# Two of four key tiles of a weighed product in high and low halves, with new places for the parts around them

## The chip, the cores and the metric

One core of a Trainium2 chip runs the whole program. The metric is the device time of one execution in microseconds (us), lower is better. Five engines work side by side, each through its own list of instructions in order: TensorE (PE, with its weight loads as PEld), VectorE (DVE), ScalarE (ACT), GpSimd (POOL) and SyncE (SP, which only issues DMAs). They wait for each other by semaphores.

## What is computed

Two layers over 8 sequences of 512 tokens of width 128. The first layer is a gated recurrence and a binarized feed-forward block. The second is a memory layer with 8 heads and a routed feed-forward block with 8 experts. The change touches the second layer's memory part, which in the reference is, cut down:

```
grads    = vmap(grad(chunk_loss))(mem_ws, keys, lr, values)     # 8 chunks of 64 tokens a head
momentum = assoc_scan(mom_gate, -grads)
updates  = assoc_scan(1 - decay, momentum)
w0, w1   = mem_w0 + updates[0], mem_w1 + updates[1]             # one pair of weights per chunk
x        = q @ w0
vals     = silu(x) @ w1
vals     = rmsnorm(vals) * (gamma + 1) * gate
out      = vals @ w_combine
```

A chunk's weights are sums of outer products of earlier tokens, so `q @ w0` is computed as the product with the start weights plus `(q k') * coef` applied to the tokens' gradients: a score matrix of keys against queries, weighed by a factor for each pair of chunks, and then "applied" as a product with a 128-row tile of gradients. Only queries behind the keys count, so key tile i (of 4 tiles of 128) needs 450 - 128 i query columns: 450, 322, 194 and 66.

## The kernel before

`first_layer` takes the first 127 us. `attend` then goes through 64 pairs (sequence, head) in `heads`, which calls `step(f, s, z)` on each engine: `f` is head n in its first half, `s` head n-1 in its second half, and `z` head n-2, whose result is added up. The order on each engine is the order of the code in its `step`. For 40 of the 64 steps (`s` in sequences 2 to 6) there is also one block `x` of 128 routed tokens through an expert. These are block steps; the other 24 are plain steps.

On TensorE a step is, in order: the projections U, EB and QA; the second scores of s; (block) a transpose of the block's rows; the product of s with `w1` into EB; `xs` with `w1` into VB and `apply(VB, err_t, ...)`, four products; (block) the first expert products; four transposes of `err`; the error product (`err_2` with `w4t`, into U); the first scores of f, with four transposes of `du` among them; the projection into XB and `apply(XB, du_t, ...)`; (block) the second expert products; `vals` with `w_out`; and the sums of squares.

A float32 matrix product is done in one of two ways here. A plain float32 `matmul` shows as two records in the trace. A `product` takes both operands as two parts of type float32r, high (a rounded copy) and low (the rest), and does high x high, low x high and high x low, one record each. Both `apply` calls are of the first kind: `p_sb` is the weighed score matrix that `weigh` on VectorE writes from PSUM (four operations of 512, 384, 128 and 256 columns, tile order 0, 1, 3, 2; `SC_BANKS` = 3 increments of `v_p1` or `v_p0`), and `err_t` and `du_t` are the transposed gradients that ScalarE copies out of PSUM.

The names around it: VectorE computes `q_sb` (L1109, L1111), `err_low` (L1115), `du` (L1118), the two `weigh` calls, and at the step's end the work that comes in some steps only: `coefs` (after heads 1 and 6 to 11), `blocks` (after 3), `places` (after 4), `last_sum` and `add_rows` (in the last sequence). The next step begins on VectorE with `ms` (L1074). GpSimd waits for that `ms` with `rs`, then computes `rg`, then `s_low` and `qa_low` (L1207), and later the two parts of the sum of squares, `sq_rest` (L1232) and `sq_low` (L1236). TensorE's product of s with `w1` waits for `s_low`, its error product for `err_low`.

Of the kernel before, what the change touches and what calls it, by code (L numbers as in the profile page):

```python
# [8 lines left out]
I32 = mybir.dt.int32  # L9
# [6 lines left out]
P = 128  # L16
# [11 lines left out]
E = 8  # L28
# [601 lines left out]
def attend(nc, m, a, out):  # L630

    with ExitStack() as ctx:
# [11 lines left out]
        err_t = sb("err_t", [P, T, D])  # L644
        du = sb("du", [P, S])
        du_t = sb("du_t", [P, T, D])
        p_sb = sb("p_sb", [P, P_COLS])
# [3 lines left out]
        sq_rest = sb("sq_rest", [P, QW])  # L651
# [6 lines left out]
        token_q = sb("token_q", [P, 3, NT])  # L658
# [4 lines left out]
        def carve(ap, at):  # L663
# [35 lines left out]
        a_sh, a_qh, a_eh, a_xh, a_hi, a_mid = (sem(f"a_{k}") for k in ("sh", "qh", "eh", "xh", "hi", "mid"))  # L699
        v_q, v_g, v_du, v_p0, v_p1, v_ms, v_acc, v_y, v_xl, v_el = (  # L700
            sem(f"v_{k}") for k in ("q", "g", "du", "p0", "p1", "ms", "acc", "yb", "xl", "el"))
        g_rs, g_rg, g_sl, g_ql, g_rest, g_lo = (sem(f"g_{k}") for k in ("rs", "rg", "sl", "ql", "rest", "lo"))
# [40 lines left out]
        with nc.Block() as block_:  # L743

            @block_.tensor
            def _(pe):
# [21 lines left out]
                def apply(out, rows, made, n):  # L768
                    for i in SC_ORDER:
                        if i != 3:  # L770
                            pe.wait_ge(made, SC_BANKS * n + {0: 1, 1: 2, 2: 3}[i])
                        last = pe.matmul(out[:, P * i:QW], rows[:, i, :], p_sb[:, P_COL[i]:P_COL[i] + QW - P * i],  # L772
                                         start=False, stop=True, skip_group_check=True)
                    return last

                def routing(s):
# [8 lines left out]
                    if c == 5:  # L785
                        pe.wait_ge(v_alpha, 1)
                        rows = FREE[:, 0:3 * NT].rearrange("p (a n) -> p a n", a=3)
                        pe.matmul(rows, m.ahead, m.per_token[:], start=True, stop=False)
                        pe.matmul(rows[:, :, 0:NT - 1], m.behind, m.per_token[:, :, 1:], start=False, stop=True).then_inc(p_shift, 1)

                def step(f, s, z):
# [27 lines left out]
                    if s is not None:  # L819
                        pe.wait_ge(v_acc, k)  # L820
                        pe.wait_ge(a_et, k + 1)
                        product(VB[:, 0:QW], [w[:] for w in w1], [part[:] for part in xs_2])
                        apply(VB, err_t, v_p1, k).then_inc(p_v, 1)
                    if x is not None:
# [4 lines left out]
                        last.then_inc(p_h, 1)  # L829
                    if f is not None:  # L830
# [4 lines left out]
                        last.then_inc(p_et, 1)  # L835
                        pe.wait_ge(v_el, n + 1)
# [14 lines left out]
                        pe.wait_ge(a_et, n + 1)  # L851
                        project(XB, m.w_x, f, SHIFT)
                        pe.wait_ge(a_dt, n + 1)
                        apply(XB, du_t, v_p0, n).then_inc(p_x, 1)
# [6 lines left out]
                    if s is not None:  # L861
                        pe.wait_ge(a_v, k + 1)
                        for t, r in enumerate(Q_ROWS):
                            pe.matmul(VB[0:r, t * P:t * P + P], vals[:, t * P:t * P + r], m.w_out[:, s[1], :], start=True, stop=True)  # L864
                        pe.wait_ge(g_lo, k + 1)
# [12 lines left out]
            def _(act):  # L878
                def gate_rows(c):
                    act.wait_ge(v_f, c + 1)  # L880
                    for t in range(T):
# [4 lines left out]
                def scale_rows(c):  # L886

                    act.wait_ge(v_top, 1)
                    for t in range(c * T, c * T + T):
# [3 lines left out]
                def spread(b):  # L893

                    for g in range(2):
                        nc.scalar.copy(gates_x[b % 2][g], gates[:, g, b * H:b * H + H, :].unsqueeze(2).broadcast_to([P, H, T, NC])).then_inc(a_gates, 1)

                def step(f, s, z):
# [7 lines left out]
                    if f is not None:  # L906
# [5 lines left out]
                        act.wait_ge(v_g, n)  # L912
                        nc.scalar.activation(th[:], U[:], ACT.Tanh, scale=0.5).then_inc(a_th, 1)
# [7 lines left out]
                        nc.scalar.copy(qa_2[0][:], qa[:]).then_inc(a_qh, 1)  # L921
                        act.wait_ge(p_e, n + 1)
                        act.wait_ge(p_d, n)
                        nc.scalar.copy(err[:], EB[:]).then_inc(a_err, 1)  # L924
                        act.wait_ge(a_err, n + 1)
                        nc.scalar.copy(err_2[0][:], err[:]).then_inc(a_eh, 1)
                    if s is not None:
                        act.wait_ge(p_v, k + 1)
# [481 lines left out]
```

## Time and profile before

| what | us |
|---|---|
| runs | 1109.14, 1114.12, 1114.44 (median 1114.12) |
| the profiled execution: time | 1113.32 |
| its span (first to last instruction) | 1110.8 |
| TensorE busy | 1071.7 (96%) |
| VectorE busy | 686.0 (62%) |
| ScalarE busy | 678.7 (61%) |
| GpSimd busy | 562.4 (51%) |
| one block step | 15.72 |
| one plain step | 13.73 |

The execution's time is 2.5 us above the span. Matmul records overlap in the trace: each lasts some 0.16 us longer than the distance to the next one, so costs on TensorE are read from the distance of starts, not from durations. A step's length is the distance of two starts of the first projection (`w_u_high`).

### The profile page before, as it was taken

The page shows a single profiled execution, that of the slowest core. Times are in us where ns is not written, and L with a number is a line of the kernel's source. Part 1 is how long each engine was busy: PE and PEld are TensorE (multiplying, and loading weights), DVE is VectorE, ACT ScalarE, POOL GpSimd, SP SyncE. Part 2 cuts the span into 40 slices and gives each one's busy share as a digit, 9 for nine tenths or more (in the row PEclk, how much of TensorE's full clock was granted, in tenths as well). Part 3 has the DMA queues.
Part 4 walks back from the last instruction along what each step waited for, and adds up shares of the span by engine and source line. Part 5 has one row for each costly group of instructions (what it writes and reads, how often), then busy time and mean ns, then how long its engine had stood idle before and what let it go on. Part 6 is the DMA issues. An engine that isn't in the chain of part 4 may idle for free. (4 is left out here: it accounts for less than half of the span.)

```text
span 1110.8 us, 19052 instructions
## 1 busy us (share of the span) xinstructions
PE 1071.7 (96%) x6613; PEld 900.1 (81%) x6613; DVE 686.0 (62%) x1752; ACT 678.7 (61%) x1356; POOL 562.4 (51%) x574
## 2 busy tenths in 40 slices
PE   6899799999999999999999999999999999999994
PEld 4666588888888888888888888888888888888883
DVE  5887566767766555565556555565556555657774
ACT  5776466677655656565556555665566565656663
POOL 6885244478874444344434444444434443444553
PEclk9999699999999999999999999999999999999997
DMA  7210300000030000000000000000000000012221
GB/s 205 79 46 29 105 1 1 1 15 30 21 97 12 19 10 9 8 21 10 9 8 11 20 11 8 9 20 11 8 8 11 20 8 6 6 42 61 69 70 42
DMA packets 42129, 32.66 MB, mean 29 GB/s; under 512 B 4042, under 2 KB 36652, under 8 KB 41900
## 3 DMA queue, kind: packets, MB, share of 16 engines
q1 hardware_dynamic: 38484, 25.93, 8.0%
q0 software_dynamic: 2304, 4.74, 1.3%
q8 instruction: 54, 0.88, 0.3%
q10 hardware_dynamic: 1248, 0.79, 0.2%
q14 instruction: 39, 0.32, 0.1%
HBM read 18.30 MB, written 13.41 MB: 29 GB/s over the span
## 5 line engine op out<-in xcount | busy, mean ns | idle before, releaser
L1040 DVE TENSOR_TENSOR p_sb<-bank,coef 128x512 f32<-128x512 f32 (+3 forms) x512 | 218.8, 483 | 3.1 <-PE bank L749 2.6
L1232 POOL TENSOR_TENSOR sq_rest<-sq,sq_high 128x450 f32<-128x450 f32 x64 | 67.2, 1050 | 245.1 <-ACT sq_high L934 245.1
L772 PE MATMUL bank<-p_sb,err_t 128*128 128x450 f32 (+3 forms) x512 | 132.9, 402 | 0.2 <-DVE p_sb L1040 0.2
L772 PE MATMUL bank<-p_sb,du_t 128*128 128x450 f32 (+3 forms) x512 | 128.8, 394 | 0.0
L772 PEld LDWEIGHTS bank<-p_sb,err_t 128*128 128x128 f32 x512 | 83.7, 190 | 45.5 <-DVE p_sb L1040 25.2
L1236 POOL TENSOR_TENSOR sq_low<-sq_rest,sq_mid 128x450 bf16<-128x450 f32 x64 | 67.6, 1056 | 96.5 <-ACT sq_mid L948 96.2
L772 PEld LDWEIGHTS bank<-p_sb,du_t 128*128 128x128 f32 x512 | 82.1, 190 | 41.4 <-issue 23.9
L1093 DVE SCALAR_TENSOR_TENSOR acc<-bank,rg,acc 128x128 f32<-128x128 f32 x224 | 62.9, 343 | 68.2 <-POOL rg L1220 68.2
L1118 DVE SCALAR_TENSOR_TENSOR du<-q_sb,bank 128x512 f32<-128x512 f32 x64 | 44.0, 688 | 87.7 <-PE bank L749 87.7
L1216 POOL TENSOR_TENSOR rs<-ms,neg_half 128x4 f32<-128x4 f32 x64 | 80.6, 1259 | 28.6 <-DVE ms L1075 27.3
L1207 POOL TENSOR_TENSOR s_low<-s_sb,s_high 128x512 fp32r<-128x512 f32 x64 | 82.7, 1293 | 20.2 <-ACT s_high L911 20.1
L909 ACT ACTIVATE s_sb<-bank 128x512 f32<-128x512 f32 x64 | 38.3, 598 | 88.4 <-PE bank L749 88.3
L903 ACT ACTIVATE xs<-bank 128x450 f32<-128x450 f32 x64 | 35.0, 547 | 89.0 <-PE bank L772 89.0
L930 ACT COPY vals<-bank 128x450 f32<-128x450 f32 x64 | 34.3, 536 | 89.3 <-PE bank L772 89.3
L1126 DVE TENSOR_TENSOR xl_all<-bank,xl_all 128x128 f32<-128x128 f32 x40 | 11.7, 293 | 117.2 <-PE bank L858 117.2
L1246 POOL DMA_INDIRECT ffn_rows<-xl_all,ids x40 | 41.5, 1039 | 83.9 <-DVE xl_all L1126 83.9
L1207 POOL TENSOR_TENSOR qa_low<-qa,qa_high 128x450 fp32r<-128x450 f32 x64 | 74.5, 1165 | 12.3 <-ACT qa_high L921 12.0
L924 ACT COPY err<-bank 128x512 f32<-128x512 f32 x64 | 37.6, 587 | 62.6 <-PE bank L749 62.6
L864 PE MATMUL bank<-w_out,vals 128*128 128x128 f32 (+1 forms) x512 | 67.4, 274 | 0.6 <-ACT vals L930 0.6
L864 PEld LDWEIGHTS bank<-w_out,vals 128*128 128x128 f32 (+1 forms) x512 | 60.0, 179 | 0.9 <-ACT vals L930 0.9
L945 ACT COPY du_t<-bank 128x512 f32<-128x512 f32 x64 | 37.6, 587 | 36.2 <-PE bank L848 36.2
L764 PE MATMUL bank<-qa,yb 128*128 128x66 f32 (+1 forms) x256 | 52.9, 288 | 0.0
(297 smaller groups left out, 3103.1 us busy)
## 6 DMA issues: line engine op xcount, KB each, us to landing
sorted_rows<-coef SPq DMA_DIRECT2D x5, 516.0 KB, 5.0
rows<-sorted_rows SPq DMA_DIRECT2D x40, 64.5 KB, 1.8
x<-in_L_attn_inputs SPq DMA_DIRECT2D x8, 256.0 KB, 5.5
x_rows<-x SPq DMA_DIRECT2D x8, 256.0 KB, 2.3
ew<-in_L_ffn_w SPq DMA_DIRECT2D x8, 256.0 KB, 3.9
attn_out<-acc SPq DMA_DIRECT2D x7, 256.0 KB, 2.1
ew<-attn_out SPq DMA_DIRECT2D x7, 256.0 KB
ew<-ffn_rows SPq DMA_DIRECT2D x8, 192.0 KB
```

What stands on the lines that cost most here:

```text
L764: last = pe.matmul(out, left[:, (i - 2) * P:(i - 1) * P], right[:, P * i:], start=True, stop=True)
L772: last = pe.matmul(out[:, P * i:QW], rows[:, i, :], p_sb[:, P_COL[i]:P_COL[i] + QW - P * i], start=False, stop=True, skip_group_check=True)
L864: pe.matmul(VB[0:r, t * P:t * P + P], vals[:, t * P:t * P + r], m.w_out[:, s[1], :], start=True, stop=True)
L909: nc.scalar.activation(s_sb[h % 2][:], U[:], ACT.Silu).then_inc(a_s, 1)
L1040: last = nc.vector.tensor_tensor(dst, src, w, ALU.mult)
L1093: last = nc.vector.scalar_tensor_tensor(sums, o, g, sums, ALU.mult, ALU.add)
L1118: nc.vector.scalar_tensor_tensor(du[:], q_sb[:], 0.5, U[:], ALU.mult, ALU.mult).then_inc(v_du, 1)
L1207: nc.gpsimd.tensor_tensor(parts[1][:], whole[:], parts[0][:], ALU.subtract).then_inc(done, 1)
L1216: nc.gpsimd.tensor_tensor(rs[:], ms[:], m.neg_half[:, 0:T], ALU.pow).then_inc(g_rs, 1)
L1232: nc.gpsimd.tensor_tensor(sq_rest[:], sq[:], sq_3[0][:], ALU.subtract).then_inc(g_rest, 1)
L1236: nc.gpsimd.tensor_tensor(sq_3[2][:], sq_rest[:], sq_3[1][:], ALU.subtract).then_inc(g_lo, 1)
L1246: nc.gpsimd.indirect_dma_start(m.ffn_rows, bass.IndirectOffsetOnAxis(ids[r][:, 0:1], axis=0), y[r], None).then_inc(s_y[r], 16)
```

## The change

- `apply` is gone. `apply_plain` does key tiles 3 and 2 as before (full float32). `apply_halves` does tiles 0 and 1 in halves: for each, high p with high and low rows, then low p with high rows.
- New operations per head and side (there are two sides, err with `v_p1` and du with `v_p0`): ScalarE makes the high parts of `p_sb` (450 and 322 columns, `p_high_of`). The low parts come from GpSimd on the err side (semaphore `g_l1`) and from VectorE on the du side (`p_low_of`, `v_l0`). `err_t` and `du_t` are split: tiles 2 and 3 stay float32, tiles 0 and 1 become pairs `errt2` and `dut2`. For `errt2` ScalarE first copies PSUM into `th`, and at the end of its step makes the high part; VectorE makes the low part (`v_etl`).
- On TensorE the transposes of `err` stand between the narrow and the halved tiles on the err side, and the output rows (`vals` with `w_out`) on the du side. The block's first expert products stand ahead of `apply_plain`.
- `du` is now `err`'s buffer, `sq_rest` is `sq`, `token_q` and `per_token` lie in `amd`. ScalarE's row work (`gate_rows`, `scale_rows`) is cut in two pieces, and the first two scatters of GpSimd come after the new low parts. `ids` moves towards the end of VectorE's step.

The diff, cut to its core:

```diff
+                def apply_plain(out, rows, made, n):
+
+                    pe.wait_ge(made, SC_BANKS * n + 3)
+                    for i in (3, 2):
+                        pe.matmul(out[:, P * i:QW], rows[:, i - 2, :], p_sb[:, P_COL[i]:P_COL[i] + QW - P * i],
+                                  start=False, stop=True, skip_group_check=True)
+
+                def apply_halves(out, halves, n, high, low, lows):
+
+                    for i in (0, 1):
+                        cols = QW - P * i
+                        p_high, p_low = (part[:, QW * i:QW * i + cols] for part in p_2)
+                        pe.wait_ge(high, 2 * n + i + 1)
+                        if lows == 3:
+                            pe.wait_ge(low, 3 * n + 1)
+                        for rows in halves:
+                            pe.matmul(out[:, P * i:QW], rows[:, i, :], p_high, start=False, stop=True, skip_group_check=True)
+                        pe.wait_ge(low, lows * n + lows - 1 + i)
+                        last = pe.matmul(out[:, P * i:QW], halves[0][:, i, :], p_low, start=False, stop=True, skip_group_check=True)
                     return last
...
+                def p_high_of(made, n, i, done):
+
+                    cols = QW - P * i
+                    act.wait_ge(made, SC_BANKS * n + i + 1)
+                    nc.scalar.copy(p_2[0][:, QW * i:QW * i + cols], p_sb[:, P_COL[i]:P_COL[i] + cols]).then_inc(done, 1)
...
                         nc.scalar.copy(qa_2[0][:], qa[:]).then_inc(a_qh, 1)
+                    if s is not None:
+                        p_high_of(v_p1, k, 0, a_p1)
+                    if f is not None:
                         act.wait_ge(p_e, n + 1)
                         act.wait_ge(p_d, n)
                         nc.scalar.copy(err[:], EB[:]).then_inc(a_err, 1)
+                    if s is not None:
+                        p_high_of(v_p1, k, 1, a_p1)
...
                         weigh(f, p_s0, v_p0, n, s)
+                        dve.wait_ge(a_dt, n + 1)
+                        nc.vector.tensor_tensor(du_t2[1][:].rearrange("p t d -> p (t d)"), EB[:, 0:2 * D],
+                                                du_t2[0][:].rearrange("p t d -> p (t d)"), ALU.subtract).then_inc(v_l0, 1)
+                        p_low_of(a_p0, n, 0, v_l0)
+                        p_low_of(a_p0, n, 1, v_l0)
+                        dve.wait_ge(a_et, 2 * n + 2)
+                        flat = [part[:].rearrange("p t d -> p (t d)") for part in err_t2]
+                        nc.vector.tensor_tensor(flat[1], th[:, 0:2 * D], flat[0], ALU.subtract).then_inc(v_etl, 1)
...
+                        for i in (0, 1):
+                            cols = QW - P * i
+                            high, low = (part[:, QW * i:QW * i + cols] for part in p_2)
+                            pool.wait_ge(a_p1, 2 * k + i + 1)
+                            nc.gpsimd.tensor_tensor(low, p_sb[:, P_COL[i]:P_COL[i] + cols], high, ALU.subtract).then_inc(g_l1, 1)
```

TensorE in a block step, from the product of `xs` with `w1` (`xs_high` against `w1n_high`) to the error product (`err_high` against `w4t_high`). Before:

```order
L749 MATMUL bank<-xs_high,w1n_low 128x450
L772 MATMUL bank<-p_sb,err_t 128x450 [waits v_p1]
L772 MATMUL bank<-p_sb,err_t 128x322 [waits v_p1]
L772 MATMUL bank<-p_sb,err_t 128x66
L772 MATMUL bank<-p_sb,err_t 128x194 [waits v_p1]
L828 MATMUL bank<-xl_all 128x128 [waits a_qa,v_xf]
L828 MATMUL bank<-xl_all 128x128 x3
L834 MATMUL bank<-ident,err 128x128 [waits a_xs,a_err]
L834 MATMUL bank<-ident,err 128x128 x3
L749 MATMUL bank<-err_high,w4t_high 128x512 [waits v_q,v_el]
```

The same stretch now:

```order
L749 MATMUL bank<-xs_high,w1n_low 128x450
L839 MATMUL bank<-xl_all 128x128 [waits a_qa,v_xf]
L839 MATMUL bank<-xl_all 128x128 x3
L772 MATMUL bank<-p_sb,err_t 128x66 [waits v_p1]
L772 MATMUL bank<-p_sb,err_t 128x194
L847 MATMUL bank<-ident,err 128x128 [waits a_xs,a_err]
L847 MATMUL bank<-ident,err 128x128 x3
L784 MATMUL bank<-p_high,errt_high 128x450 [waits a_p1,v_etl]
L784 MATMUL bank<-p_high,errt_low 128x450
L786 MATMUL bank<-p_low,errt_high 128x450 [waits g_l1]
L784 MATMUL bank<-p_high,errt_high 128x322 [waits a_p1]
L784 MATMUL bank<-p_high,errt_low 128x322
```

The halved tiles stand right ahead of the error product, and the expert products that stood behind the applies stand ahead of them.

GpSimd in the same step, where `s_low` and `qa_low` are what TensorE needs early and `ffn_rows` is the block's result. Before:

```order
L1216 TENSOR_TENSOR rs<-ms,neg_half 128x4 [waits v_ms]
L1220 TENSOR_TENSOR rg<-rs,lr_gate 128x4 [waits v_acc,g_rs]
L1207 TENSOR_TENSOR s_low<-s_sb,s_high 128x512 [waits a_sh]
L1207 TENSOR_TENSOR qa_low<-qa,qa_high 128x450 [waits a_qh]
L1232 TENSOR_TENSOR sq_rest<-sq,sq_high 128x450 [waits p_o,a_hi]
L1236 TENSOR_TENSOR sq_low<-sq_rest,sq_mid 128x450 [waits g_rest,a_mid]
```

Now:

```order
L1279 TENSOR_TENSOR rs<-ms,neg_half 128x4 [waits v_ms]
L1283 TENSOR_TENSOR rg<-rs,lr_gate 128x4 [waits v_acc,g_rs]
L1270 TENSOR_TENSOR s_low<-s_sb,s_high 128x512 [waits a_sh]
L1270 TENSOR_TENSOR qa_low<-qa,qa_high 128x450 [waits a_qh]
L1295 TENSOR_TENSOR p_low<-p_sb,p_high 128x450 [waits a_p1]
L1295 TENSOR_TENSOR p_low<-p_sb,p_high 128x322 [waits a_p1]
L1301 TENSOR_TENSOR sq<-sq,sq_high 128x450 [waits p_o,a_hi]
L1305 TENSOR_TENSOR sq_low<-sq,sq_mid 128x450 [waits g_rest,a_mid]
```

Two operations have come in between `qa_low` and the squares.

VectorE at the end of the same step and the start of the next, from the last weighed tile to `ms`. Before:

```order
L1040 TENSOR_TENSOR p_sb<-bank,coef 128x256 [waits p_s0]
L1126 TENSOR_TENSOR xl_all<-bank,xl_all 128x128 [waits p_yy]
L1067 TENSOR_LOAD blk_e
L1067 ISA x2
L1069 ISA [waits v_yx]
L1069 COPY xl_all<-ew 128x646
L1074 TENSOR_SCALAR ms<-bank 128x3 [waits g_rs,p_o]
```

Now:

```order
L1087 TENSOR_TENSOR p_sb<-bank,coef 128x256 [waits p_s0]
L1176 TENSOR_TENSOR dut_low<-bank,dut_high 128x256 [waits a_dt]
L1097 TENSOR_TENSOR p_low<-p_sb,p_high 128x450 [waits a_p0]
L1097 TENSOR_TENSOR p_low<-p_sb,p_high 128x322 [waits a_p0]
L1182 TENSOR_TENSOR errt_low<-thu,errt_high 128x256 [waits a_et]
L1187 COPY ids<-rows 128x1 [waits s_y0,s_rows0]
L1189 TENSOR_TENSOR xl_all<-bank,xl_all 128x128 [waits p_yy]
L1122 TENSOR_LOAD blk_e
```

Four operations stand between `weigh` and the step's end. In a plain step the blocks' rows are absent, and `coefs` or one of the others follows the fourth.

## Rows read from the trace of the kernel before

**Rows 1.** The page: busy time by engine, and TensorE's granted clock in 40 slices.

```profile
PE 1071.7 (96%) x6613; PEld 900.1 (81%) x6613; DVE 686.0 (62%) x1752; ACT 678.7 (61%) x1356; POOL 562.4 (51%) x574
...
PEclk9999699999999999999999999999999999999997
```

**Rows 2.** Windows: stretch, length, busy time (x instructions) of the engines, PEclk, DMA.

```profile
503.80:519.52 15.72, 15.72 (x107) 13.55 (x105) 8.93 (x24) 9.30 (x19) 6.98 (x8) 1.00 0.03 9
266.25:279.98 13.73, 13.73 (x91) 11.67 (x88) 10.19 (x21) 8.87 (x18) 11.39 (x12) 1.00 0.06 20
```

**Rows 3.** Timeline of PE in one block step: start us, us, engine, line, operation.

```profile
503.80 0.48 PE L749 MATMUL bank<-y_high,w_u_high 128*128 128x512 f32 x1
...
508.33 0.36 PE L749 MATMUL bank<-xs_high,w1n_high 128*128 128x450 f32 x1
508.53 0.37 PE L749 MATMUL bank<-xs_low,w1n_high 128*128 128x450 f32 x1
...
508.97 2.12 PE L772 MATMUL bank<-p_sb,err_t 128*128 128x450 f32 x8
...
512.17 0.48 PE L749 MATMUL bank<-err_high,w4t_high 128*128 128x512 f32 x1
...
513.57 0.31 PE L749 MATMUL bank<-qa_high,y_high 128*128 128x322 f32 x1
513.71 0.31 PE L749 MATMUL bank<-qa_low,y_high 128*128 128x322 f32 x1
...
515.57 2.01 PE L772 MATMUL bank<-p_sb,du_t 128*128 128x450 f32 x8
```

**Rows 4.** The same timeline, cut behind the fourth record of the du apply.

```profile
515.57 1.46 PE L772 MATMUL bank<-p_sb,du_t 128*128 128x450 f32 x4
```

**Rows 5.** Timeline of DVE in the same block step.

```profile
508.23 1.68 DVE L1040 TENSOR_TENSOR p_sb<-bank,coef 128x512 f32<-128x512 f32 x4
509.82 0.68 DVE L1109 SCALAR_TENSOR_TENSOR q_sb<-bank,s_sb 128x512 f32<-128x512 f32 x1
510.54 0.69 DVE L1111 SCALAR_TENSOR_TENSOR q_sb<-thu,q_sb 128x512 f32<-128x512 f32 x1
511.15 0.68 DVE L1115 TENSOR_TENSOR err_low<-err,err_high 128x512 fp32r<-128x512 f32 x1
```

**Rows 6.** Timelines of POOL and ACT in the same block step.

```profile
506.11 1.29 POOL L1207 TENSOR_TENSOR s_low<-s_sb,s_high 128x512 fp32r<-128x512 f32 x1 [0.19 <-ACT s_high L911]
507.64 1.15 POOL L1207 TENSOR_TENSOR qa_low<-qa,qa_high 128x450 fp32r<-128x450 f32 x1 [0.23 <-ACT qa_high L921]
...
506.99 0.57 ACT L921 CAST qa_high<-qa 128x450 fp32r<-128x450 f32 x1
```

**Rows 7.** Timelines of POOL and DVE in a plain step, where the two overlap.

```profile
229.70 1.15 POOL L1207 TENSOR_TENSOR qa_low<-qa,qa_high 128x450 fp32r<-128x450 f32 x1
...
229.41 0.68 DVE L1109 SCALAR_TENSOR_TENSOR q_sb<-bank,s_sb 128x512 f32<-128x512 f32 x1
230.12 1.29 DVE L1111 SCALAR_TENSOR_TENSOR q_sb<-thu,q_sb 128x512 f32<-128x512 f32 x1
```

**Rows 8.** Timelines at the step's end with `places`: DVE, then POOL, then PE.

```profile
206.34 0.16 DVE L1015 TENSOR_TENSOR ew<-ew 128x8 f32<-128x8 f32 x1
...
210.95 0.15 DVE L1074 TENSOR_SCALAR ms<-bank 128x3 f32<-128x3 f32 x1
...
212.80 1.27 POOL L1207 TENSOR_TENSOR s_low<-s_sb,s_high 128x512 fp32r<-128x512 f32 x1
...
209.48 0.47 PE L749 MATMUL bank<-y_high,w_u_high 128*128 128x512 f32 x1
...
214.12 0.50 PE L749 MATMUL bank<-s_high,w1n_high 128*128 128x512 f32 x1 [0.39 <-POOL s_low L1207]
```

**Rows 9.** Timelines of DVE with `coefs`, `blocks` and `last_sum`.

```profile
263.11 0.68 DVE L985 TENSOR_TENSOR_SCAN ew<-ew 128x256 f32<-128x256 f32 x1
263.83 1.48 DVE L987 TENSOR_TENSOR_SCAN coef<-ew 128x256 f32<-128x256 f32 x1
...
192.62 0.68 DVE L1003 TENSOR_TENSOR_SCAN ew<-restart,ew 128x256 f32<-128x256 f32 x1
...
196.08 0.16 DVE L1074 TENSOR_SCALAR ms<-bank 128x3 f32<-128x3 f32 x1
...
1058.13 1.92 DVE L1157 SCALAR_TENSOR_TENSOR ew<-ew,token_q 128x128 f32<-128x128 f32 x4
```

More of the change, by code:

```diff
@@ L643, in attend @@
         err, err_2 = sb("err", [P, S]), pair("err2", [P, S])
[L644 to L647, printed above, removed]
+        err_t, err_t2 = sb("err_t", [P, 2, D]), pair("errt2", [P, 2, D])
+        du = err
+        du_t, du_t2 = sb("du_t", [P, 2, D]), pair("dut2", [P, 2, D])
+        p_sb, p_2 = sb("p_sb", [P, P_COLS]), pair("p2", [P, 2 * QW - P])
         xs, xs_2 = sb("xs", [P, QW]), pair("xs2", [P, QW])
@@ L787, in routing @@
                         rows = FREE[:, 0:3 * NT].rearrange("p (a n) -> p a n", a=3)
-                        pe.matmul(rows, m.ahead, m.per_token[:], start=True, stop=False)
+                        pe.matmul(rows, m.ahead, m.per_token, start=True, stop=False)
                         pe.matmul(rows[:, :, 0:NT - 1], m.behind, m.per_token[:, :, 1:], start=False, stop=True).then_inc(p_shift, 1)
@@ L884, in gate_rows, with scale_rows @@
                     last.then_inc(a_g, 1)
-                def scale_rows(c):
+                def scale_rows(c, tiles):
                     act.wait_ge(v_top, 1)
-                    for t in range(c * T, c * T + T):
+                    for t in (c * T + t for t in tiles):
                         last = nc.scalar.mul(m.xl_all[:, t, 0:D], m.xl_all[:, t, 0:D], m.rr[:, 2, t:t + 1])
@@ L896, in spread, with rows_of @@
                         nc.scalar.copy(gates_x[b % 2][g], gates[:, g, b * H:b * H + H, :].unsqueeze(2).broadcast_to([P, H, T, NC])).then_inc(a_gates, 1)
+                def rows_of(s, tiles):
+                    k, c = n_of(s), last_head(s)
+                    if c is not None and c > 0:
+                        gate_rows(c - 1, tiles)
+                    if 1 <= k <= B:
+                        scale_rows(k - 1, tiles)
                 def step(f, s, z):
@@ L924, in step @@
                         nc.scalar.copy(err[:], EB[:]).then_inc(a_err, 1)
+                    if s is not None:
+                        p_high_of(v_p1, k, 1, a_p1)
+                    if f is not None:
                         act.wait_ge(a_err, n + 1)
                         nc.scalar.copy(err_2[0][:], err[:]).then_inc(a_eh, 1)
+                    if x is not None:
+                        act.wait_ge(p_h, x + 1)
+                        for k4 in range(FB):
+                            last = nc.scalar.activation(hid[:, k4, :], QA[:, k4 * P:k4 * P + P], ACT.Relu, bias=w1s[:, PAR + 2 + k4:PAR + 3 + k4])
+                        last.then_inc(a_h, 1)
                     if s is not None:
+                        rows_of(s, (0, 1))
                         act.wait_ge(p_v, k + 1)
@@ L1042, in weigh, with p_low_of @@
                             last.then_inc(done, 1)
+                def p_low_of(made, n, i, done):
+                    cols = QW - P * i
+                    p = p_sb[:, P_COL[i]:P_COL[i] + cols]
+                    dve.wait_ge(made, 2 * n + i + 1)
+                    high, low = (part[:, QW * i:QW * i + cols] for part in p_2)
+                    nc.vector.tensor_tensor(low, p, high, ALU.subtract).then_inc(done, 1)
                 def plain_keys(b):
@@ L1167, in finish_batch @@
                     q = (B - 1) % 2
[L1168 removed]
+                    dve.wait_ge(a_g, 2 * B)
                     dve.wait_ge(v_acc, B * H)
```

89 lines of the change are left out of this document (46 added, 43 removed).

## The prediction, made before the changed kernel had run

> **What bounds the kernel now.** I read the page first. TensorE is busy for 96% of the span at the full clock, the other engines for 51 to 62% [rows 1]. The windows say the same of one step: in a block step TensorE is busy for all of 15.72 us, in a plain one for all of 13.73, and PEclk is 1.00 in both [rows 2]. So a microsecond taken off TensorE counts, as long as nobody else comes late. The slack of the others has to be read from their order, not from their busy share. One wait is visible on TensorE: the err apply is 2.12 long where the same eight records on the du side are 2.01 [rows 3], so some 0.13 in each block step goes into waiting for the first weighed tile (0.03 in a plain one).
>
> I take times in a block step from its first projection, at 503.80 [rows 3].
>
> **TensorE's own work.** Tiles 0 and 1 of one apply are four records: 1.46 less the tail of 0.16 (a 450-column record lasts 0.37 where the next begins 0.20 later [rows 3, 4]) is 1.30 us. A float32r product of 450 columns takes 0.20 to 0.205 and one of 322 takes 0.15 [rows 3], three of each are 1.065. That saves 0.23 per apply, 0.46 per step, **29.4 us over 64 steps**. Tiles 2 and 3 stay as they are, and no product is added elsewhere. The weight loads go from two to three per tile, and each lies beside a product of at least 0.15.
>
> **Small waits.** On the err side `apply_plain` now wants all four weighed tiles. They end at 509.91, which is 6.11 [rows 5]; TensorE, which now does the block's 0.89 us first, comes at 6.03, so 0.13 remains. On the du side the last weighed tile needs scores that end only 0.6 us earlier, so some 0.05 is new. Plain steps get 0.05 there and some 0.14 at the halved du tiles. Against before that is +0.05 per block step and +0.16 per plain step: **+5.8 us**.
>
> **The low parts on GpSimd.** This is the term that I expect to decide. In a block step the first weighed tile is done at 5.11, ScalarE's high part takes the 0.57 of `qa_high` [rows 6] and is there at 5.73, and GpSimd's low part at 1.15 for 450 columns runs from 5.77 to 6.92 [rows 6]. The second, 322 columns, is 1.15 less 128 x 0.0022 (the slope between 1.29 for 512 and 1.15 for 450 [rows 6]), 0.88. VectorE at that time does the second `q_sb` (from 6.74) and `err_low` (from 7.35) [rows 5]. Both read two tensors from SBUF, and so does GpSimd. What happens then is in the trace: `q_sb` takes 0.69 alone [rows 5], but 1.29 when it starts at 230.12 while GpSimd's `qa_low` runs from 229.70 to 230.85 [rows 7]. It ends 0.56 after GpSimd's end, that is it did its work only once GpSimd let go, 0.13 before its end. The first `q_sb`, which reads PSUM, took its usual 0.68 beside it [rows 7]. There are eight such steps.
>
> So the four operations go one after the other: GpSimd 450 until 6.92; `q_sb` until 7.48; GpSimd 322 (held back until 0.13 before that) until 8.25; `err_low`, which asks last, until 8.80. If GpSimd's second came ahead of `q_sb`, the sum and the end would be nearly the same (8.9). TensorE would be at its error product at 8.22 (8.45 before, less 0.23) and gets `err_low` at 8.87: a wait of 0.65 in each of 40 block steps, **+26 us**. The low part itself, at 8.30, lies within that. In a plain step the products come 0.89 earlier and GpSimd follows `qa_low` at once: low part until 6.1, `q_sb` until 6.65, low part until 7.4, `err_low` until 7.97, TensorE would be there at 7.13 and waits 0.91: 24 x 0.91, **+21.8 us**. Bounds: nothing, if the operations overlap freely (`err_low` is then ready at 8.03, as before), and 0.8 per block step and 1.1 per plain step if the order is the worst. I take the worked values, since the eight rows show the same engines, the same operations and the same sizes.
>
> The Trainium skill says the same kind of thing more strictly: SBUF — State Buffer, section "Who interferes with whom", holds that a VectorE instruction with two SBUF inputs and a GpSimd instruction that reads SBUF exclude each other for the whole instruction. By that the 0.13 of overlap at each of three handovers is lost too, and the sum would be some 25 us higher; the row shows the 0.13, and I go by the row.
>
> **The end of VectorE's step.** New there are four operations after `weigh`: 256 columns, 450, 322 and 256, about 0.42 + 0.62 + 0.54 + 0.49. They wait for ScalarE's high parts, which stand behind `sq_mid`, and the 450 one meets GpSimd's `sq_low` as above. Laid out, a plain step's last one ends 0.15 us before the step does; before, `weigh` ended about 3 us before. In block steps there are 1.1 us more (the second expert products and the rest), so nothing is late there. In plain steps whatever follows is pushed into the next step: `coefs` 2.15 (7 steps), `blocks` 3.46 (1), `places` 4.6 (1) [rows 8, 9], `last_sum` 1.92 (7), with `add_rows` and its wait 2.5 (6 of those 7). Behind them stand `ms`, then GpSimd's `rs`, `rg` and `s_low`, for which TensorE waits. The trace has one such case: with `places` `ms` came 1.47 after the step's first projection, `s_low` ended at 214.07, and TensorE lost 0.98 by then [rows 8]. So the loss is `ms`'s delay less 0.5, and it spares 0.2 of the wait at `err_low`. With the delay equal to the work less 0.15: coefs 1.3 x 7 = 9.0, blocks 2.6, places 3.75 - 0.98 = 2.8, last_sum alone 1.0, with add_rows 1.6 - 0.29 = 1.3 x 6 = 7.8. Together **+23 us** (15 to 32; none, if VectorE's end came over 2.5 us sooner than I lay it out).
>
> **Ends.** In the first step `choose` is pushed back by 2, in the last the halves come one after another, +1: **+3 us**.
>
> **The sum.** 1113.3 - 29.4 + 5.8 + 26 + 21.8 + 23.2 + 3 = 1163.7 for the profiled execution's time (its span is 2.5 less). The median is 0.8 above that execution, so I say 1164. Its own range is 1140 to 1182.
>
> **Rivals.** (1) TensorE stays the bound everywhere: the four operations overlap, and the end of VectorE's step is absorbed. For it speaks that every engine has several us of idle time in a step [rows 2]; against it the 1.29 of rows 7. It gives 1113.3 - 29.4 + 5.8 = 1090 (1084 if the small waits go as well). (2) No exclusion at `err_low`, but the end of the step works as laid out, without the meeting with `sq_low`: 1113.3 - 29.4 + 5.8 + 22 + 3 = 1115, no change. It turns slower than before where the pushed work exceeds 20 us. (3) Exclusion as forecast, but the pushed work finds room: 1113.3 + 24.2 + 3 = 1140. That holds if `sq_mid` and ScalarE's high parts come 1 us sooner. (4) The halved tiles don't run as one-record products at 0.205. The saving is then gone and everything else stands: over 1190. The existing products are of just this form, so this is unlikely.
>
> **How the numbers follow.** Forecast 0.50, rival 3 (still slower) 0.16, rival 2 0.14, rival 1 0.16, rival 4 and worse 0.04. Rival 2 lies half within 0.5% and half to its sides (0.5% is about what a measurement of this kernel can tell from no change): same 0.09, faster 0.18, slower 0.73. The range of 8 in 10 leaves out rival 1 and the worst: 1106 to 1184.
>
> **What would show it.** Right: the second `q_sb` or `err_low` with means well over 0.69 and 0.68, idle time of TensorE ahead of `w4t_high` released by `err_low` (0.65 per block step, 0.9 per plain one), block steps of 15.9 to 16.0 and plain ones of 14.3, and steps of over 15.5 after heads 6 to 11 and 57 to 62 with TensorE waiting for `s_low`. Wrong: block steps of 15.3 with `err_low` at 0.68 (rivals 1 and 2), no idle time ahead of `s_low`'s product (rivals 1 and 3). TensorE's busy share should fall to some 90% if I am right and stay near 96% in rival 1. The forecast rests on one pair of waits; if GpSimd's low parts start 1 us sooner than I lay out, they are over before the second `q_sb`, and a block step is 0.4 shorter than before instead of 0.24 longer.

## The result

The changed kernel takes 1172.61 us (median of four runs, 1170.56 to 1172.97) against 1112.53 for the kernel before on the same chip: ratio 1.054, 95% interval 1.0508 to 1.0572. It is slower by 5.4%. The forecast was 1164, range 1106 to 1184. The profiled execution took 1172.53 us, 59.2 more than that of before (1113.32); its span is 1170.8.

### The profile after

The page's busy times and TensorE's granted clock of the changed kernel, against [rows 1]:

```profile
PE 1099.9 (94%) x6869; PEld 936.0 (80%) x6869; DVE 874.2 (75%) x2008; ACT 807.0 (69%) x1804; POOL 709.1 (61%) x702
...
PEclk9999799999999999999999999999999999999996
```

The clock is as before. TensorE has less work to do and yet more busy time, because a matmul record is drawn out to its modelled end and covers short waits. Steps tell more. The windows of a block step, a plain step, and a plain step behind `coefs` (stretch, length, busy time of PE, PEld, DVE, ACT, POOL, PEclk), against [rows 2]:

```profile
603.06:619.13 16.07, 15.94 (x111) 14.13 (x109) 11.80 (x27) 11.24 (x27) 9.37 (x10) 1.00 0.03 10
...
365.03:379.44 14.41, 14.09 (x94) 12.07 (x92) 11.66 (x24) 10.27 (x23) 8.06 (x8) 1.00 0.09 25
...
285.52:301.97 16.45, 14.85 (x94) 11.91 (x92) 13.50 (x26) 11.01 (x25) 13.57 (x14) 1.00 0.05 16
```

Block steps went from 15.72 to 16.07, plain ones from 13.73 to 14.41, the ones behind `coefs` from 13.73 to 16.45. The starts of the 64 first projections put the loss, 54.4 us from the first of them to the last, at 14.0 in the 40 block steps and 40.3 in the 23 other intervals; of these, 7.7 lie in four steps of the last sequence, which went from 14.07 to 16.0.

What TensorE's weight loads waited for over the whole run (us in total, times, longest):

```profile
PEld bank L749 <- DVE err_low L1166: 23.9, 63, 1.4
PEld bank L772 <- ACT du_t L989: 23.1, 64, 0.8
...
PEld bank L749 <- DVE ms L1130: 16.1, 12, 2.5
PEld bank L772 <- DVE p_sb L1087: 10.6, 52, 0.7
PEld bank L749 <- POOL s_low L1270: 9.5, 13, 1.0
PEld bank L786 <- DVE p_low L1097: 8.7, 22, 0.9
```

The wait for `err_low` was forecast, and the one for `s_low` behind a late `ms`. That TensorE would wait for `ms` itself, 16.1 us in 12 places, and for `du_t` was not. The groups of the two VectorE instructions that the forecast named, with GpSimd's low parts (busy us, mean ns):

```profile
L1295 POOL TENSOR_TENSOR p_low<-p_sb,p_high 128x450 fp32r<-128x450 f32 (+1 forms) x128 | 147.0, 1170 | 37.5 <-ACT p_high L903 36.1
...
L1166 DVE TENSOR_TENSOR err_low<-err,err_high 128x512 fp32r<-128x512 f32 x64 | 78.5, 1226 | 0.3 <-ACT err_high L967 0.3
...
L1162 DVE SCALAR_TENSOR_TENSOR q_sb<-thu,q_sb 128x512 f32<-128x512 f32 x64 | 53.0, 828 | 2.2
```

In a block step before, `err_low` took 0.68 and `q_sb` 0.69 [rows 5]. The timelines of the block step at 603.06, GpSimd first, then VectorE, the weight loads and TensorE (start us, us):

```profile
608.81 2.31 POOL L1295 TENSOR_TENSOR p_low<-p_sb,p_high 128x450 fp32r<-128x450 f32 x2 [0.77 <-ACT p_high L903]
...
609.76 0.75 DVE L1162 SCALAR_TENSOR_TENSOR q_sb<-thu,q_sb 128x512 f32<-128x512 f32 x1
610.43 1.24 DVE L1166 TENSOR_TENSOR err_low<-err,err_high 128x512 fp32r<-128x512 f32 x1
...
611.72 0.19 PEld L749 LDWEIGHTS bank<-err_high,w4t_high 128*128 128x128 f32 x1 [0.36 <-DVE err_low L1166]
...
611.18 0.41 PE L786 MATMUL bank<-p_low,errt_high 128*128 128x322 f32 x1
611.72 0.51 PE L749 MATMUL bank<-err_high,w4t_high 128*128 128x512 f32 x1
612.07 0.39 PE L749 MATMUL bank<-err_low,w4t_high 128*128 128x512 f32 x1
```

GpSimd's two low parts end at 611.12. `err_low` started at 610.43 and ends at 611.67, 0.55 behind them, where alone it takes 0.68. It did its work only when GpSimd was through, but for the last 0.13, as the `q_sb` of [rows 7]. TensorE had its last halved record at 611.18, could have gone on 0.15 later, and got `err_low` at 611.72.

### The profile page after: what moved, and what is told of

Read it like the earlier page. It is cut to its first block and busy times, and to the rows that moved or that the text cites. A ratio compares the mean times of both kernels' runs of the same rounds, so it can differ in the third digit from the quotient of the medians.

```text
span 1170.8 us, 20652 instructions
## 1 busy us (share of the span) xinstructions
PE 1099.9 (94%) x6869; PEld 936.0 (80%) x6869; DVE 874.2 (75%) x2008; ACT 807.0 (69%) x1804; POOL 709.1 (61%) x702
## 5 line engine op out<-in xcount | busy, mean ns | idle before, releaser
L903 ACT CAST p_high<-p_sb 128x450 fp32r<-128x450 f32 (+1 forms) x256 | 125.9, 519 | 79.9 <-DVE p_sb L1087 79.8
L1295 POOL TENSOR_TENSOR p_low<-p_sb,p_high 128x450 fp32r<-128x450 f32 (+1 forms) x128 | 147.0, 1170 | 37.5 <-ACT p_high L903 36.1
L1301 POOL TENSOR_TENSOR sq<-sq,sq_high 128x450 f32<-128x450 f32 x64 | 67.0, 1046 | 132.6 <-ACT sq_high L981 132.5
L1097 DVE TENSOR_TENSOR p_low<-p_sb,p_high 128x450 fp32r<-128x450 f32 (+1 forms) x128 | 101.5, 831 | 31.5 <-ACT p_high L903 31.3
L1305 POOL TENSOR_TENSOR sq_low<-sq,sq_mid 128x450 bf16<-128x450 f32 x64 | 66.9, 1046 | 62.6 <-ACT sq_mid L992 62.4
L1169 DVE SCALAR_TENSOR_TENSOR err<-q_sb,bank 128x512 f32<-128x512 f32 x64 | 44.0, 688 | 72.6 <-PE bank L749 72.6
L1166 DVE TENSOR_TENSOR err_low<-err,err_high 128x512 fp32r<-128x512 f32 x64 | 78.5, 1226 | 0.3 <-ACT err_high L967 0.3
L1162 DVE SCALAR_TENSOR_TENSOR q_sb<-thu,q_sb 128x512 f32<-128x512 f32 x64 | 53.0, 828 | 2.2
L772 PE MATMUL bank<-p_sb,err_t 128*128 128x66 f32 (+1 forms) x256 | 51.9, 326 | 0.1
L772 PEld LDWEIGHTS bank<-p_sb,du_t 128*128 128x128 f32 x256 | 33.4, 190 | 23.1 <-ACT du_t L989 23.1
```

What stands on the lines that cost most here:

```text
L772: pe.matmul(out[:, P * i:QW], rows[:, i - 2, :], p_sb[:, P_COL[i]:P_COL[i] + QW - P * i], start=False, stop=True, skip_group_check=True)
L903: nc.scalar.copy(p_2[0][:, QW * i:QW * i + cols], p_sb[:, P_COL[i]:P_COL[i] + cols]).then_inc(done, 1)
L1097: nc.vector.tensor_tensor(low, p, high, ALU.subtract).then_inc(done, 1)
L1166: nc.vector.tensor_tensor(err_2[1][:], err[:], err_2[0][:], ALU.subtract).then_inc(v_el, 1)
L1295: nc.gpsimd.tensor_tensor(low, p_sb[:, P_COL[i]:P_COL[i] + cols], high, ALU.subtract).then_inc(g_l1, 1)
L1301: nc.gpsimd.tensor_tensor(sq[:], sq[:], sq_3[0][:], ALU.subtract).then_inc(g_rest, 1)
```

## The experiments

All ratios are against runs of the kernel before on the same chip. "The changed kernel" is 1172.6 us. An "interval" is the distance of two starts of the first projection.

### 1. Is the wait GpSimd's doing? `err_low` from PSUM

```diff
-  nc.vector.tensor_tensor(err_2[1][:], err[:], err_2[0][:], ALU.subtract).then_inc(v_el, 1)
+  nc.vector.tensor_tensor(err_2[1][:], EB[:], err_2[0][:], ALU.subtract).then_inc(v_el, 1)
```

`EB` is the PSUM bank that `err` was copied from, so the values are the same, and the instruction has one SBUF input in place of two. First in the changed kernel, then in the kernel before.

> The changed kernel with one operand moved: err_low is computed as EB (still in PSUM) minus err_high, not err (in SBUF) minus err_high. Same values, same place, same size; it only no longer reads two tensors from SBUF. Theory (VectorE and GpSimd exclude each other when both read two SBUF tensors): err_low back from 1.24 to 0.68 us, ready about 0.55 us sooner; TensorE is then held by GpSimd's low part of tile 1 itself, so a block step falls from 16.09 to about 15.7 and a plain one from 14.4 to about 14.0. 40 x 0.4 + 24 x 0.4 = 26 us less, 1146 us, between 1138 and 1152. Rival (err_low is late because ScalarE's high parts push err_high back, or because weigh is late): nothing changes, 1172.

> The kernel before with the same one operand moved. There GpSimd is idle during err_low, so the theory expects no change: within 2 us of the kernel before, err_low at 0.68 us. A rival that reading PSUM is faster in itself would show a gain here too.

Measured: 1147.31 us, ratio 1.0302 (1.0274 to 1.0329), and 1113.61, ratio 0.9998 (0.9979 to 1.0017). The group of `err_low` in the first:

```profile
L1166 DVE TENSOR_TENSOR err_low<-bank,err_high 128x512 fp32r<-128x512 f32 x64 | 43.3, 677 | 0.0
```

One operand was changed; GpSimd's low parts ran in the same place as before (1147 and 1198 ns on average, 1146 and 1193 in the changed kernel) and VectorE's instruction went from 1226 to 677 ns beside them. In the kernel before it takes 0.683 from either source, so reading PSUM is not faster in itself. So the wait comes from two SBUF inputs meeting GpSimd, and neither from ScalarE's high parts nor from the order. It is worth 25.3 us in the changed kernel and nothing in the kernel before. Block steps fell to 15.67, plain ones to 14.0.

The timeline of TensorE in a block step of the first shows what it waits for now, and what a wait costs beside its length:

```profile
585.39 0.31 PE L784 MATMUL bank<-p_high,errt_low 128*128 128x322 f32 x1
585.54 0.41 PE L786 MATMUL bank<-p_low,errt_high 128*128 128x322 f32 x1
585.79 0.39 PE L749 MATMUL bank<-err_high,w4t_high 128*128 128x512 f32 x1
586.03 0.39 PE L749 MATMUL bank<-err_low,w4t_high 128*128 128x512 f32 x1
```

The last halved record takes 0.25 instead of 0.15, because its weight load had to wait for GpSimd's second low part and starts only as the record does, at 585.54. (In plain steps the record also starts 0.35 late.) That lay hidden in the wait for `err_low`. And the error product's first record takes 0.24 here, 0.35 where TensorE stood before it (611.72 to 612.07 above): after that wait the first record costs some 0.1 more.

I put this down to the weight load. Here it starts 0.15 ahead of its record (585.64 against 585.79), so it runs beside the record before; after the wait both start at 611.72. The kernel before shows that no wait is needed for it. There the same product stands behind four short transposes, its load starts only 0.03 ahead of the record of 512.17 [rows 3], and the record takes 0.31 with TensorE never idle:

```profile
512.14 0.19 PEld L749 LDWEIGHTS bank<-err_high,w4t_high 128*128 128x128 f32 x1
...
512.48 0.40 PE L749 MATMUL bank<-err_low,w4t_high 128*128 128x512 f32 x1
```

In the changed kernel the first halved record stands behind these transposes and takes 0.29 (610.19 to 610.48) instead of 0.205, so that cost has moved, and the 0.35 at the error product comes on top. The three pairs fit; no run changes the lead of a load by itself.

### 2. One side at a time

The err side alone: `du_t` whole again, and the old `apply` for it. The du side alone: the same for `err_t`, with no low parts on GpSimd.

```diff
-                        apply_plain(XB, du_t, v_p0, n)
+                        apply(XB, du_t, v_p0, n).then_inc(p_x, 1)
...
-                        apply_halves(XB, du_t2, n, a_p0, v_l0, 3).then_inc(p_x, 1)
```

> Only the err side (VB) is in halves; the du side is one full float32 apply at its old place, without its four VectorE operations and ScalarE copies. Theory: TensorE saves 0.23 per step, the wait at err_low stays (0.65 per block step, 0.9 per plain one), the end of VectorE's step is short again, so the steps after heads 6 to 11 and 57 to 62 lose their extra wait for s_low. 40 x 0.4 + 24 x 0.7 + 2 = 35 above before: 1148 us, block steps 16.1, plain steps 14.4, all plain steps alike within 0.4. Rival (the loss is the du side's VectorE work alone): 1105 to 1113.

> Only the du side (XB) is in halves, low parts on VectorE; the err side is one full float32 apply at its old place, without GpSimd's low parts. Theory: no wait at err_low; block steps 15.72 - 0.23 + 0.05 = 15.55, plain ones 13.7, but the pushed end of VectorE's step stays, with steps over 15 after heads 6 to 11 and 57 to 62: 1113 - 8 + 24 + 3 = 1132 us. Rival (only the exclusion costs anything, VectorE's end of the step finds room): 1113 - 15 = 1098 to 1105.

Measured: err side 1149.62 us, ratio 1.032 (1.0291 to 1.0349), with block steps of 16.07 as in the changed kernel and plain ones of 14.35. The time was as expected, but the plain steps are not alike within 0.4: 15.0 to 15.2 behind heads 7 to 10, 15.0 in the last sequence, 16.0 behind head 6 and 17.1 with `places`. I put that down to `errt_low`, the one of VectorE's four new operations that this kernel keeps. Du side 1146.11, ratio 1.0279 (1.0242 to 1.0315), 14 above what was expected, all of it in the block steps (15.97). Both sides lose by themselves. The miss on the du side has a row of its own, here the weight loads in a block step of that kernel, with ScalarE behind:

```profile
581.40 0.19 PEld L749 LDWEIGHTS bank<-y_high,w_x_high 128*128 128x128 f32 x1 [0.51 <-ACT err_t L984]
...
578.08 1.14 ACT L971 ACTIVATE xl_all<-bank,xl_all 128x128 f32<-128x128 f32 x4 [2.25 <-PE bank L849]
579.10 0.56 ACT L977 COPY vals<-bank 128x450 f32<-128x450 f32 x1
...
580.77 0.58 ACT L984 COPY err_t<-bank 128x512 f32<-128x512 f32 x1
```

ScalarE waits 2.25 for the block's first expert products (L849), to do their ReLUs, and `vals`, the squares and `err_t` queue behind them. The changed kernel can afford that order, because its TensorE does these products ahead of the err apply; my kernel had put the products back and left ScalarE's order. Two further runs follow this up.

### 3. Both leads followed up, and the wait called `du_t`

The err side alone with `err_low` from PSUM; the du side alone with the ReLUs behind the `err_t` copy as before; and the changed kernel with `err_low` from PSUM and the plain du tiles moved:

```diff
-                        pe.wait_ge(a_dt, n + 1)
-                        apply_plain(XB, du_t, v_p0, n)
...
                     if f is not None:
+                        pe.wait_ge(a_dt, n + 1)
+                        apply_plain(XB, du_t, v_p0, n)
                         apply_halves(XB, du_t2, n, a_p0, v_l0, 3).then_inc(p_x, 1)
```

> The err side alone in halves, and err_low reads the error in PSUM. In the err side alone (1149.6 us) TensorE waits 0.41 for err_low in a block step, as in the changed kernel. If that wait is the exclusion between GpSimd's low parts and a VectorE instruction with two SBUF inputs, and nothing else comes late in its place: err_low back at 0.68, block steps 15.66 instead of 16.07, plain steps 13.95 instead of 14.35, the steps after heads 6 to 11 down by about as much, and 1149.6 - 0.40 x 64 = 1124 us. If the du side were needed for the wait, 1149. The err side in halves would still be slower than the kernel before (1113): it keeps the late low part of tile 1 and its errt_low behind the weighing.

> The du side alone came to 1146.1, 14 above its expectation, all of it in the block steps (15.97 instead of 15.55). Its trace shows TensorE at the XB projection 0.51 late for ScalarE's err_t copy: ScalarE does the block's ReLUs ahead of vals there, as in the changed kernel, while TensorE still does the block's first products behind the err apply, as before. Here only that is undone: the ReLUs go behind the err_t copy again. If the miss came from this mixture, block steps are 15.55 to 15.6 and the time 1146.1 - 0.4 x 40 = 1130 us. If it came from the du side's own work (two copies on ScalarE, low parts on VectorE), it stays at 1146. What is left above 1113 - 0.2 x 64 = 1100 in the first case is the end of VectorE's step, pushed into the next one after heads 6 to 11, places and last_sum.

> Changed kernel with err_low from PSUM (1147.3), and TensorE does the plain du tiles 2 and 3 right ahead of the halved ones, behind the second expert products and the output rows. In 1147.3 TensorE waits at those plain tiles for the last weighed tile of the du side: 0.16 more between the projection's last product and the first plain record than its 0.20, in each step. If that is all that the wait costs, it goes, since the tiles are weighed 2 us earlier than they are then wanted: block steps 15.51 instead of 15.67, plain 13.85 instead of 14.0, 1147.3 - 0.16 x 64 = 1137 us. If TensorE then only waits as much longer for p_low of the du side, which is what ends last in plain steps, block steps gain and plain ones don't: 1141.

Measured: 1127.21 us, ratio 1.0117 (1.01 to 1.0133), block steps 15.67, plain 13.95, as expected step by step and 3 above in all. The GpSimd effect doesn't need the du side.

The second came to 1136.31, ratio 1.0193 (1.0176 to 1.021). The mixture explains 10 of the 14; `err_t` is ready in time and the XB projection no longer waits. But block steps are 15.72 and not 15.55 to 15.6, the same length as before, although an apply is shorter. Its weight loads say where that went:

```profile
578.99 0.52 PEld L780 LDWEIGHTS bank<-p_sb,du_t 128*128 128x128 f32 x4 [0.34 <-ACT du_t L988]
```

This is the wait that stands with 23.1 us in the list of the changed kernel. The profile names `du_t`, since one weight load has two conditions, the copy and the last weighed tile. In the changed kernel's block step the copy (ScalarE) ends at 615.06, the weighing (VectorE) at 615.17, and the load starts at 615.28:

```profile
613.42 1.75 DVE L1087 TENSOR_TENSOR p_sb<-bank,coef 128x512 f32<-128x512 f32 x4
...
614.68 0.38 ACT L989 COPY du_t<-bank 128x256 f32<-128x256 f32 x1
...
615.28 0.52 PEld L772 LDWEIGHTS bank<-p_sb,du_t 128*128 128x128 f32 x4 [0.34 <-ACT du_t L989]
...
614.96 0.37 PE L749 MATMUL bank<-y_high,w_x_low 128*128 128x450 f32 x1
615.32 0.79 PE L772 MATMUL bank<-p_sb,du_t 128*128 128x66 f32 x4
```

From the projection's last product to the first plain record it is 0.36, where the product takes 0.20: a wait of 0.16. I read it as the last weighed tile, since the copy was there 0.22 ahead and the tile 0.11; no run tells the two apart. The third kernel takes it away, whichever it is: 1138.82 us, ratio 1.0213 (1.0193 to 1.0234), 8.5 below the kernel without the move. Block steps are 15.45, 0.22 shorter, the wait and the 0.07 that the first records after it cost. The narrow tiles' own records, x4, went from 0.79 above to 0.72:

```profile
587.55 0.72 PE L772 MATMUL bank<-p_sb,du_t 128*128 128x66 f32 x4
```

Plain steps stay at 14.0: there the same time is spent at the halved tiles, where the wait for `p_low` on VectorE goes from 9.9 to 15.9 us in all. Of the two outcomes written down, the time (1137 and 1141) lies between them, the steps say the second.

### 4. Without the step's end: halves in block steps alone

What is lost outside the block steps is put down, so far by argument only, to VectorE's new work at the step's end. The last pair tests that. It puts the du side in halves in the 40 block steps alone, everything else as before, and beside it in every step. Both have the plain du tiles moved and the ReLUs as before, and the old err side.

```diff
-                    if f is not None:
+                    if f is not None and x is not None:
                         pe.wait_ge(a_dt, n + 1)
                         apply_plain(XB, du_t, v_p0, n)
                         apply_halves(XB, du_t2, d_at(n), a_p0, v_l0, 3).then_inc(p_x, 1)
```

(`x is not None` marks a block step; the same condition stands at ScalarE's high parts and VectorE's low parts.)

> Halves on the du side alone and in the 40 block steps alone, with the plain du tiles right ahead of the halved ones and the ReLUs behind the err_t copy; the err side and the 24 plain steps are the kernel before's. Where the du side was in halves in every step (1136.3), the block steps were as long as before (15.72), with 0.16 of waiting for the last weighed tile ahead of the plain tiles, and the loss of 23 us lay in the other steps: 15.1 after heads 6 to 11 and in the last sequence against 13.7 and 14.1, 17.9 against 15.2 with places. If that loss is VectorE's low parts pushing coefs, places and last_sum into the next step, it is gone here: plain steps 13.73, after heads 6 to 11 13.73, last sequence 14.07. The block steps should be 15.72 - 0.16 to 15.72 - 0.22, so 1113.4 - 40 x 0.19 = 1106 us, ratio 0.993. If the halves lose their 0.2 to another wait, 1113.

> The same with the du side in halves in every step. Block steps as in the kernel with block steps alone (15.5 to 15.56); plain steps 13.73 to 13.8, where the wait ahead of the plain tiles turns into one for the low parts; after heads 6 to 11, places and last_sum as in the du side alone (15.1, 17.9, 15.2), since nothing is taken from VectorE. So 1136.3 - 40 x 0.18 = 1129 us. The difference to the kernel with block steps alone, 23 us, would be what the end of VectorE's step costs in steps with coefs, places, blocks and last_sum. If the two come out alike, the tail is not VectorE's.

Measured: **1104.32 us, ratio 0.9911 (0.9892 to 0.9931)** for block steps alone, and 1125.08, ratio 1.0123 (1.0099 to 1.0147) for every step. The first beats both kernels of this case. A block step and a plain step behind `coefs` in it, as windows:

```profile
549.53:565.03 15.50, 15.50 (x110) 13.79 (x107) 10.85 (x26) 10.16 (x23) 7.07 (x8) 1.00 0.04 8
267.55:281.26 13.71, 13.71 (x90) 11.69 (x88) 9.99 (x21) 8.85 (x18) 11.48 (x12) 1.00 0.06 20
```

Its block steps are 0.23 shorter than before, what was worked out for one apply, with no wait in between. The two kernels have the same block steps (15.5), so the 20.8 us between them (18.9 between the two profiled executions) lie in the other steps, 19.0 by the intervals: with halves in all of them, 15.1 to 15.5 behind `coefs` against 13.7 to 14.0, 17.8 against 15.7 with `places`, 15.2 against 14.05 in the last sequence. A plain step without extra work is 13.8 against 13.73, so the halves cost next to nothing there by themselves; where more work follows them on VectorE, they cost 1.1 to 2.2 (some 0.1 only behind heads 1 and 11).

How, the changed kernel's step from 285.52 to 301.97 shows. VectorE's timeline from its low parts on, then the weight loads that wait, at the end of this step and in the next, and TensorE's record behind the last wait:

```profile
299.18 2.03 DVE L1097 TENSOR_TENSOR p_low<-p_sb,p_high 128x450 fp32r<-128x450 f32 x2 [0.55 <-ACT p_high L903]
301.13 1.67 DVE L1182 TENSOR_TENSOR errt_low<-thu,errt_high 128x256 fp32r<-128x256 f32 x1
302.72 0.68 DVE L1032 TENSOR_TENSOR_SCAN ew<-ew 128x256 f32<-128x256 f32 x1
303.44 0.69 DVE L1034 TENSOR_TENSOR_SCAN coef<-ew 128x256 f32<-128x256 f32 x1
304.05 0.13 DVE L1129 TENSOR_SCALAR ms<-bank 128x3 f32<-128x3 f32 x1
...
300.86 0.19 PEld L786 LDWEIGHTS bank<-p_low,dut_high 128*128 128x128 f32 x1 [0.72 <-DVE p_low L1097]
...
304.29 0.19 PEld L749 LDWEIGHTS bank<-y_high,w_qk_high 128*128 128x128 f32 x1 [1.11 <-DVE ms L1130]
...
307.24 0.50 PE L749 MATMUL bank<-s_high,w1n_high 128*128 128x512 f32 x1 [0.45 <-POOL s_low L1270]
```

`ms` comes 2.08 after the step's first projection at 301.97, where it is 0.17 otherwise. TensorE stands still three times: for the du side's own low part (held up beside `sq_low`), for `ms` ahead of its third projection, and for `s_low`. And GpSimd in the same stretch:

```profile
299.25 1.06 POOL L1305 TENSOR_TENSOR sq_low<-sq,sq_mid 128x450 bf16<-128x450 f32 x1
300.48 1.19 POOL L1262 DMA_INDIRECT sorted_rows<-xl_all,place  x1 [0.17 <-issue]
301.70 0.81 POOL L1266 TENSOR_TENSOR ew<-lr_gate,starts 128x256 f32<-128x256 f32 x1
```

The low parts of the du side meet `sq_low`, and `errt_low`, 0.41 long in a block step, takes 1.67: it ends 0.29 behind GpSimd's `starts` (302.51).

## Why the prediction held, and where its steps were off

The time was in the range and the sign was right, 8.6 us above the number. That it came so close is in part luck: by the table the terms are off by +13.7, -7.3 and +2.4 us, which partly cancel. The sum of its terms, against what the step of 603.06, the two plain steps from 1037.42 and the intervals show (us; per step in brackets, block and plain):

| term | forecast | measured |
|---|---|---|
| TensorE's work | -29.4 (-0.46, -0.46) | -0.23 for one apply in experiment 4, taken as -29.4 |
| small waits | +5.8 (0.05, 0.16) | +19.5 (0.32, 0.28) |
| wait at `err_low` | +47.8 (0.65, 0.91) | +40.5 (0.49, 0.87) |
| end of the step, ends | +26.2 | +28.6 (what is left of 59.2) |

- **TensorE's work.** Right: 450 and 322 columns take 0.205 and 0.15 as halves, and experiment 4 shows 0.23 for the du side's apply with nothing in its way. The err side's is taken to be the same.
- **The wait at `err_low`.** The mechanism is shown by experiment 1, and the order laid out ahead came true: `q_sb` ends at 7.45 in the step (forecast 7.48), GpSimd's second low part at 8.06 (8.25), `err_low` at 8.61 (8.80). All of the difference is in the 322 columns, which took some 0.7 once `q_sb` let go and not the 0.88 worked out by the slope. TensorE could have been there at 8.27 (611.18 plus 0.15) and starts at 8.66, so the wait is 0.39, and 0.1 for the first record. In the plain step below it is 0.74 and 0.1: the last halved record starts 0.35 late for GpSimd, the error product as much again for `err_low`. "The low part itself lies within that" was right, and is why taking `err_low` away gave 25 and not 40. The timeline of TensorE there:

```profile
1044.23 0.31 PE L784 MATMUL bank<-p_high,errt_low 128*128 128x322 f32 x1
1044.73 0.41 PE L786 MATMUL bank<-p_low,errt_high 128*128 128x322 f32 x1 [0.18 <-POOL p_low L1295]
1045.27 0.50 PE L749 MATMUL bank<-err_high,w4t_high 128*128 128x512 f32 x1
1045.61 0.40 PE L749 MATMUL bank<-err_low,w4t_high 128*128 128x512 f32 x1
```

- **Small waits.** This is the term that was mis-sized. "Some 0.05 is new" on the du side is 0.16 and 0.07; and at the narrow err tiles the 0.13 of waiting stays, as written, but the first records after it now cost 0.09 more than before. Left out was what a wait costs beside its length, some 0.1 for a weight load that no longer runs beside a record. (The 0.28 of plain steps is what their 0.69 leaves when the other terms are taken off; 0.22 of it is again the du side's.)
- **The end of the step.** `places` cost 3.0 more than other steps do (forecast 2.8), `add_rows` steps 1.25 (1.3 forecast), `blocks` 1.7 (2.6), `last_sum` alone nothing (1.0). Five of the seven steps behind `coefs` cost 2.0 to 2.1 more where 1.3 was forecast for all seven; the one behind head 11 costs 0.9 and the one behind head 1 some 0.4. The path was only half forecast. The prediction named `s_low` alone, but in the step from 301.97 TensorE loses 0.83 ahead of its third projection, waiting for `ms`, and 0.63 ahead of the product that needs `s_low`; the forecast's "delay less 0.5" held both, because it was read from the start of that product. Two of its numbers there have errors of opposite sign: VectorE's end comes 0.83 after the step's end, not 0.15 ahead of it, because `errt_low` meets GpSimd too, which was not in the forecast; and the pushed scans take 1.33 and not 2.15, because they run where GpSimd is idle.
- **Rivals.** 1 and 2 (no exclusion) fall with experiment 1. 3 (the pushed work finds room) falls with the 16.45 of the steps behind `coefs` and the 20.8 us of experiment 4. 4 falls with the 0.205.
- **What was to show it.** `q_sb` and `err_low` at 0.83 and 1.23, block steps 16.07 (15.9 to 16.0), plain ones 14.4 (14.3), steps of 16.0 to 16.8 behind `coefs` and in the last sequence: as named, but for the step behind head 11, which is 15.3. The idle time put down to `err_low` ahead of `w4t_high` is 0.36 in block steps and in plain ones, not 0.65 and 0.9: in plain steps as much again is lost one record earlier, for GpSimd's low part. TensorE's busy share went to 94% and not to "some 90%": the share can't be used for waits of a few tenths.

Of the two views on how strictly GpSimd and VectorE exclude each other, the row's was the better one. The Trainium skill (SBUF — State Buffer, "Who interferes with whom") has the instructions exclude each other for their whole length. `err_low` ends 0.55 behind GpSimd and takes 0.68 alone, so 0.13 of it overlapped again; the forecast's alternative of 25 us more would have been 1189.

**What stays open.** Whether the 0.16 ahead of the narrow du tiles is the copy's or the weighing's. And both sides in halves in block steps alone, with `err_low` from PSUM, wasn't tried. From the block step of experiment 3 (15.45 with both sides, 15.50 with the du side) I estimate that 2 us are to be had there.

## What to carry to other kernels

Shortening the busiest engine's work by moving conversions to the others pays only where their results are ready: lay out each helper's operations in time, and see which of them read SBUF at the same time, before counting what the busiest engine saves. Where one of two partners of such a meeting can read PSUM in place of the SBUF copy, that is one operand, and it cost nothing here (0.9998 in the kernel before). And a change that gains in one kind of step and loses in another should be made in the first kind alone: for the du side that turned +1.2% into -0.9%. (From the changed kernel's +5.4% it also took leaving out the err side and moving the plain tiles and the ReLUs.)

## What the runs showed of the hardware that I had not expected

- After a wait, TensorE's first record costs 0.07 to 0.12 more than in a running stream: 0.35 against 0.24 at the error product. Behind short transposes it costs 0.31 with no wait at all (experiment 1).
- In the block steps the two engines took turns: GpSimd's first low part, `q_sb`, GpSimd's second (1.21 from its start, ending 0.6 behind `q_sb`'s end), `err_low`. This is also the order in which they started, so "whoever comes first" fits as well as taking turns. It is no rule for all cases: in the step above, `errt_low` starts at 301.13 and waits through the rest of GpSimd's indirect DMA (to 301.67) and all of `starts` (to 302.51), though `p_low` of 322 columns took its usual 0.48 beside the same indirect DMA. Why is open.
- The `coef` scan takes 0.69 with GpSimd idle (above) and 1.48 in [rows 9], from 263.83 to 265.31. GpSimd's `sq_low` ran beside it there, and the scan ends 0.56 behind it, as `q_sb` does in [rows 7]:

```profile
263.70 1.05 POOL L1236 TENSOR_TENSOR sq_low<-sq_rest,sq_mid 128x450 bf16<-128x450 f32 x1
```

That fits a scan that reads SBUF being held up by GpSimd in the same way; it was not tested by itself.
